# Rows gathered by index tile by tile, and attention heads in 8 and 16 bits over 128-row keys

## The chip, the cores and the metric

One core of one Trainium2 chip runs the whole kernel in one launch. The metric is the device time of that launch in microseconds; the kernel before takes 337.29 us (median of three runs, 334.5 to 338.93). The core has five engines with queues of their own that meet only at semaphores: PE (TensorE), DVE (VectorE), ACT (ScalarE), POOL (GpSimd) and SP (SyncE, which here issues DMAs only).

## The reference

Four residual blocks over x of 1024 tokens by 256; ctx is 4 x 256 x 256.

```python
x = x + experts(layernorm(x), token_ids, Wg=Wu=Wd=ctx)     # expert of a token from its id, clipped, // 3125
#   g = silu(h @ ctx[e].T); u = h @ ctx[e].T; y = (g * u) @ ctx[e].T
x = x + fp8(layernorm(x)) @ fp8(W8).T * scales              # e4m3, one scale per tensor, result in bf16
h = layernorm(x)
q = fq_sym(h @ Wq + bq, per head row); k, v = fq_sym(ctx @ Wkv + bkv)   # 16 heads of 16, 1024 keys, 8-bit grids
p = softmax(q k^T / 4); p = round(p / (max p / 255)) * (max p / 255)
x = x + (p @ v) @ Wp + bp
x = x + layernorm(x) @ ternary(Wt).T + bt
```

The probabilities are integers from 0 to 255 times a scale, so they can be held in 16 bits or in 8.

## The kernel before, in words

The order of all work is written out by hand: each engine has one block, and what an engine does next is the next line of its block, held back by `wait_ge` on semaphores.

**Sorting (0 to 36 us).** Tokens are counted per expert by small matmuls over masks, which give each token its place (`dest`). The token rows are loaded into `record`, POOL scatters them to a buffer in HBM in eight indirect DMAs (L369), and one DMA loads the sorted rows into `xs` (L314). PE meanwhile turns ctx and makes keys and values `kv` (L1022), DVE adds their bias (L695). The first layer norm follows for all eight tiles at once: sums on DVE (L684), root on POOL (L374, L375), norm on DVE (L703).

**Experts (36 to 86 us).** Eleven jobs: eight tiles of 128 sorted tokens, and three extra jobs for tiles in which an expert begins. A step of the loop over `s` holds, for different jobs, a transpose (L1039), the gate product (L1047), a sigmoid on ACT, two products on DVE (`zz`, `gu`), a transpose back (L1080), the second product, and the addition to `xs`. Between them DVE's `background(s)` prepares keys, values and weights, and the second norm's sums follow. POOL splits the keys into bf16 parts; its last product (`ksplit`, L401) signals `klo`, upon which SP turns the keys by eight DMA transposes into `keysT` (L321), where head 2j holds rows 0 to 63 and head 2j+1 rows 64 to 127.

**fp8 block and queries (86 to 129 us).** A maximum over all, quantising on DVE, a product, the third norm's sums (L850), its root on POOL (L374, four tiles at a time), norms, query products (L1158), their 8-bit grid, and transposes into `qT`.

**Attention (129 to 302 us).** For each of eight tiles and 16 heads: PE makes 128 x 1024 scores in two matmuls over the head's 64 rows (L1175) in one of three PSUM buffers, DVE reduces their maximum (L878), POOL makes the bias of the exponential (L421), ACT writes exp as int16 and its sum (L566), and so frees the buffer. For every pair of heads SP issues a DMA transpose of 2048 columns into `probT` (L331), and PE weighs the values, eight matmuls per head (L1204), six heads behind the scores. Once a tile DVE divides (L923), and POOL adds the output bias `bp` to a tile (L432) and copies the tile's scales to `qcur`.

**End (302 to 336 us).** Projection, fourth norm, ternary product, and eight scatters of the output.

## Time and profile before

| | us |
|---|---|
| runs: median (lowest to highest) | 337.29 (334.5 to 338.93) |
| profiled execution | 337.5 |
| its span, first to last instruction | 335.7 |
| PE / DVE / ACT / POOL busy | 268.7 / 265.7 / 210.0 / 98.3 |
| mean granted TensorE clock | 0.65 of full |

Busy time says how much of the span an engine computes, not which one holds up the others: PE and DVE are both near 80%. The strips of the page divide the span into 40 slices of 8.4 us; a digit 5 in the clock strip is the lower of TensorE's two levels (1.2 GHz), a 9 the upper one (2.4 GHz). The timeline gives each instruction's start and length, and in brackets how long its engine had been idle and what it waited for.

### The profile page before, as it was taken

The page shows a single profiled execution, that of the slowest core. Times are in us where ns is not written, and L with a number is a line of the kernel's source. Part 1 is how long each engine was busy: PE and PEld are TensorE (multiplying, and loading weights), DVE is VectorE, ACT ScalarE, POOL GpSimd, SP SyncE. Part 2 cuts the span into 40 slices and gives each one's busy share as a digit, 9 for nine tenths or more (in the row PEclk, how much of TensorE's full clock was granted, in tenths as well). Part 3 has the DMA queues.
Part 4 walks back from the last instruction along what each step waited for, and adds up shares of the span by engine and source line. Part 5 has one row for each costly group of instructions (what it writes and reads, how often), then busy time and mean ns, then how long its engine had stood idle before and what let it go on. Part 6 is the DMA issues. An engine that isn't in the chain of part 4 may idle for free.

```text
span 335.7 us, 5142 instructions
## 1 busy us (share of the span) xinstructions
PE 268.7 (80%) x1728; PEld 127.3 (38%) x1728; DVE 265.7 (79%) x401; ACT 210.0 (63%) x340; POOL 98.3 (29%) x225
## 2 busy tenths in 40 slices
PE   4993597595156947899999999999999999979670
PEld 4441365473034733233333332333333333338560
DVE  3363799968697878999999899899999999973850
ACT  1100125435533178999999999999999999992210
POOL 2350424476603011221222212222222122211634
PEclk9999559987555977555555555555555555558998
DMA  7824000039100001999999999999999999995011
GB/s 255 276 94 126 0 3 0 0 59 161 34 0 0 0 2 37 196 182 206 185 200 178 215 172 212 184 212 164 227 167 219 197 188 190 199 184 109 16 49 63
DMA packets 148618, 43.34 MB, mean 129 GB/s; under 512 B 143216, under 2 KB 147696, under 8 KB 148592
## 3 DMA queue, kind: packets, MB, share of 16 engines
q1 hardware_dynamic: 146496, 39.60, 65.4%
q0 software_dynamic: 768, 2.10, 1.8%
q10 hardware_dynamic: 1328, 1.32, 1.2%
q8 instruction: 14, 0.23, 0.3%
q14 instruction: 12, 0.10, 0.1%
HBM read 5.25 MB, written 2.10 MB: 22 GB/s over the span
## 4 chain that ended last, share of the span: by engine, by line
issue 36%; DVE 18%; PE 17%; POOL 16%; ACT 6%; DMA 6%; POOLq 1%; ACTq 0%; DVEq 0%
POOL ebias L421 8%; PE ps L1175 5%; PE ps L1158 4%; PE ps L1047 3%; DMA ksplit<-in_x 3%; DVE nmax L878 2%; ACT ctxT L566 2%; POOL scratch L369 2%; PE ps L1150 2%; POOL rstd L375 2%; POOL xs L432 2%; DMA xs<-scratch 2%; POOL out L446 1%; DVE stats L850 1%; ACT kv L557 1%
## 5 line engine op out<-in xcount | busy, mean ns | idle before, releaser
L878 DVE TENSOR_REDUCE nmax<-ps 128x1 f32<-128x1024 f32 x128 | 156.3, 1224 | 16.5 <-PE ps L1175 11.6
L1175 PE MATMUL ps<-keysT,kv 64*128 64x512 bf16 x256 | 130.1, 614 | 9.2 <-ACT ctx L566 1.9
L566 ACT ACTIVATE ctx<-ps,ebias,qscale 128x1024 int16<-128x1024 f32 x64 | 76.9, 1203 | 5.4 <-POOL ebias L421 3.5
L566 ACT ACTIVATE ctxT<-ps,ebias,qscale 128x1024 int16<-128x1024 f32 x64 | 77.0, 1203 | 4.0 <-POOL ebias L421 2.5
L1204 PEld LDWEIGHTS ps<-vals,ksplit 128*128 128x128 f16 x1024 | 36.9, 105 | 100.6 <-issue 100.3
L421 POOL TENSOR_SCALAR ebias<-nmax,qcur 128x1 f32<-128x1 f32 x128 | 33.8, 264 | 136.2 <-DVE nmax L878 127.2
L1204 PE MATMUL ps<-vals,ksplit 128*128 128x16 f16 x1024 | 47.7, 176 | 0.8 <-DVE krest L923 0.8
L475 ACT COPY hT<-ps 128x256 f32<-128x256 f32 x11 | 4.1, 372 | 46.5 <-PE ps L1039 46.5
L1175 PEld LDWEIGHTS ps<-keysT,kv 64*128 64x128 bf16 x256 | 16.3, 107 | 21.8 <-ACT ctx L566 8.1
L543 ACT COPY hT<-ps 128x512 f32<-128x512 f32 x8 | 4.7, 586 | 22.5 <-PE ps L1150 22.5
L1022 PE MATMUL ps<-wkv_s,ctxT 128*128 128x512 f32 x32 | 16.4, 668 | 0.7 <-ACT ctxT L469 0.7
L374 POOL TENSOR_SCALAR vareps<-mv 128x1 f32<-128x1 f32 (+3 forms) x15 | 3.9, 257 | 44.3 <-DVE mv L854 29.8
L1047 PE MATMUL ps<-ctxT,hT 128*128 (+1 forms) x44 | 15.5, 486 | 1.7 <-ACT hT L475 1.7
L1047 PE MATMUL ps<-ctxT,guT 128*128 (+1 forms) x44 | 13.3, 431 | 1.3 <-ACT guT L481 1.3
L375 POOL TENSOR_TENSOR rstd<-vareps,half 128x1 f32<-128x1 f32 (+3 forms) x15 | 12.5, 834 | 1.3
L566 ACT ACTIVATION_READ_ACCUMULATOR ctx<-ps,ebias,qscale 128x1 f32 x64 | 12.3, 192 | 0.0
L566 ACT ACTIVATION_READ_ACCUMULATOR ctxT<-ps,ebias,qscale 128x1 f32 x64 | 12.2, 191 | 0.0
L1047 PEld LDWEIGHTS ps<-ctxT,hT 128*128 128x128 f32 x44 | 10.2, 246 | 4.4 <-issue 2.8
L369 POOL DMA_INDIRECT scratch<-ksplit,dest x8 | 7.9, 992 | 12.3 <-DMA ksplit<-in_x 10.1
L695 DVE TENSOR_TENSOR kv<-ps,bkv_b 128x512 f32<-128x512 f32 x8 | 5.3, 683 | 7.3 <-PE ps L1022 6.6
L1039 PE MATMUL ps<-identf,hs 128*128 128x128 f32 x16 | 3.9, 331 | 8.8 <-DVE hs L703 8.8
L1080 PE MATMUL ps<-identf,gu 128*128 128x128 f32 x22 | 5.2, 324 | 7.0 <-DVE gu L768 7.0
(176 smaller groups left out, 316.1 us busy)
## 6 DMA issues: line engine op xcount, KB each, us to landing
ctx<-in_ctx SPq DMA_DIRECT2D x2, 512.0 KB, 4.9
ksplit<-in_x ACTq DMA_DIRECT2D x1, 1024.0 KB, 10.9
xs<-scratch SPq DMA_DIRECT2D x1, 1024.0 KB, 5.6
wkv_s<-in_L_xattn_Wkv SPq DMA_DIRECT2D x1, 512.0 KB, 8.1
ksplit<-ctx SPq DMA_TRANSPOSE x32, 4.7
ksplit<-ctxT SPq DMA_TRANSPOSE x32, 4.9
bkv_b<-in_L_xattn_bkv ACTq DMA_DIRECT2D x1, 256.0 KB, 11.4
wt_s<-in_L_ffn_weight SPq DMA_DIRECT2D x1, 256.0 KB, 9.4
```

The costliest lines, as they stand in the source:

```text
L369: g.indirect_dma_start(scratch, bass.IndirectOffsetOnAxis(ap=dest[:, t:t + 1], axis=0), record[:, t, :], None).then_inc(scattered, 16)
L375: root = g.tensor_tensor(rstd[:, lo:hi], vareps[:, lo:hi], half[:, 0:hi - lo], ALU.pow)
L421: g.tensor_scalar(ebias[:, slot], nmax[:, slot], qcur[:, u:u + 1], LN255, ALU.mult, ALU.add).then_inc(bias_ready, 1)
L432: g.tensor_tensor(xs[:, t, :], xs[:, t, :], bp_b[:, :], ALU.add).then_inc(x3b_ready, 1)
L566: a.activation(prob_of(w)[:, (u % 2) * NK:(u % 2 + 1) * NK], score_banks(k, u), ACT.Exp, bias=ebias[:, u % 4:u % 4 + 1], scale=qscale[:, t ...
L878: v.tensor_reduce(nmax[:, u % 4:u % 4 + 1], score_banks(k, u), AX.X, ALU.max, negate=True).then_inc(max_ready, 1)
L1022: last = m.matmul(ps[:, KVB[r % 4], :], ctxT[:, c, r * P:(r + 1) * P], wkv_s[:, c, :], start=(c == 0), stop=(c == C - 1))
L1047: last = m.matmul(ps[:, bank, 0:D], lhs[:, c, :], ctxT_e[:, c, e, :], start=(c == 0), stop=(c == C - 1))
L1150: last = m.transpose(ps[:, bank, k * P:(k + 1) * P], src[:, t, c * P:(c + 1) * P], identf[:, :])
L1158: last = m.matmul(ps[:, bank, i * D:(i + 1) * D], lhs[:, g % 2, i * C + c, :], w[:, c, :], start=(c == 0), stop=(c == C - 1))
L1175: last = m.matmul(ps[:, bank + b, :], qT[rows, t, u // 2, :], keysT[rows, u // 2, 512 * b:512 * b + 512], start=True, stop=True)
L1204: last = m.matmul(out, probT[:, (u // 2) % PAIRS, (u % 2) * KT + r, :].bitcast(F16), vals[:, r, u * HD:(u + 1) * HD], start=(r == 0), stop ...
```

## The change

It has four parts.

1. *Rows by index.* A second set of small matmuls turns `dest` into its inverse, `token_of`: the token at each sorted place. POOL then gathers `xs` tile by tile straight from x; load, scatter and reload are gone. The first norms are done tile by tile, three on DVE and five on ACT, and the experts start while kv products are still to come. ACT makes z squared beside the sigmoid, so one product on DVE gives the gate. The jobs are ordered five tiles, three extras, three tiles.
2. *8/16-bit heads.* The exponentials of even heads are written as bytes, two keys to a 16-bit word (so ACT reads PSUM with a step of 128 elements), those of odd heads as int16. A pair is then 1536 columns for the DMA transpose. POOL copies an even head's transposed bytes into 16-bit words (`byteT`, `unpack`), six heads behind, and PE weighs seven heads behind.
3. *Keys of 128 rows.* Each block of keys is turned twice into `keysT[:, a]`, and POOL clears the half that belongs to the other head of the pair (`keys_zeroed`), so that scores take all 128 rows. The roots of the third norm stand behind this on POOL. `klo` stands behind the second norm's roots.
4. *Unread transposes.* Before each head's weighing PE makes four 128 x 128 transposes of the identity into a free half of a bank that nobody reads (`FILLERS`). The output bias is added in two instructions ahead of the loop, and `qcur` is gone.

```diff
-FIRST_MAINS = 3
+FIRST_MAINS = 5
+EARLY_NORMS = 3
+ROOT_GROUPS = ((0, 1), (1, 3), (3, 5), (5, 7), (7, 8))
 QT_BY_DVE = (5, 7)
-KEY_PARTS = (4, 6)
-NORM_AT = 4
+KEY_PARTS = (7, 10)
+KV_FIRST = 5
 PARTS = 3
 PAIRS = 4
-WEIGH_LAG = 6
+PT = 4
+UNPACK_LAG = 6
+WEIGH_LAG = 7
+FILLERS = 4
...
-                sp.dma_start_transpose(keysT[:, :, r * P:(r + 1) * P],
-                                       ksplit[:, r * H:(r + 1) * H, :, :].rearrange("p a s d -> p (a s d)")).then_inc(
-                                           keys_turned[r], 16)
+                for a in range(2):
+                    sp.dma_start_transpose(keysT[:, a, :, r * P:(r + 1) * P],
+                                           ksplit[:, r * H:(r + 1) * H, :, :].rearrange("p a s d -> p (a s d)")).then_inc(
+                                               keys_turned[r], 16)
...
-            pool.wait_ge(dest_ready, 1)
-            pool.wait_ge(ld_x, 16)
-            for t in range(NT):
-                g.indirect_dma_start(scratch, bass.IndirectOffsetOnAxis(ap=dest[:, t:t + 1], axis=0),
-                                     record[:, t, :], None).then_inc(scattered, 16)
+            def gather(t):
+                g.indirect_dma_start(xs[:, t, :], None, x_rows,
+                                     bass.IndirectOffsetOnAxis(ap=token_of[:, t:t + 1], axis=0)).then_inc(gathered[t], 16)
...
+            pool.wait_ge(token_ready, 1)
+            for t in range(3):
+                gather(t)
+            for k, (lo, hi) in enumerate(ROOT_GROUPS):
+                first_root(lo, hi)
+                for t in range(2 * k + 3, min(2 * k + 5, NT)):
+                    gather(t)
...
+            for t in range(0, NT, 2):
+                pool.wait_ge(sums2_ready, t + 2)
+                inverse_root(t, t + 2)
+                for i in range(t, t + 2):
+                    g.tensor_scalar(nmr[:, i:i + 1], mv[:, i, 0:1], rstd[:, i:i + 1], -1.0,
+                                    ALU.mult, ALU.mult).then_inc(rstd2, 1)
             pool.wait_ge(kmid, 2)
             g.tensor_tensor(ksplit[:, :, 2, :], k3, ksplit[:, :, 1, :], ALU.subtract).then_inc(klo, 1)
-            for t in range(NT):
-                pool.wait_ge(sums2_ready, t + 1)
-                inverse_root(t, t + 1)
-                g.tensor_scalar(nmr[:, t:t + 1], mv[:, t, 0:1], rstd[:, t:t + 1], -1.0,
-                                ALU.mult, ALU.mult).then_inc(rstd2, 1)
             pool.wait_ge(wide_used, 5)
             g.tensor_tensor(vq[:, :, :], kv[:, :, D:2 * D],
                             vinv[:, :].unsqueeze(1).broadcast_to([P, KT, D]), ALU.mult).then_inc(vn_ready, 1)
 
+            pool.wait_ge(vn_ready, 1)
+            for r in range(KT):
+                pool.wait_ge(keys_turned[r], 32)
+                for a in range(2):
+                    if r + a:
+                        pool.wait_ge(keys_zeroed, 2 * r + a)
+                    other = slice(P // 2, P) if a == 0 else slice(0, P // 2)
+                    g.memset(keysT[other, a, :, r * P:(r + 1) * P].bitcast(F32), 0.0).then_inc(keys_zeroed, 1)
+
+            pool.wait_ge(keys_zeroed, 2 * KT)
...
+            def unpack(t, u):
+
+                pair_turned(pool, t, u // 2)
+                if not (first_tile(t) and u < 2 * PT):
+                    pool.wait_ge(pv_done, count(*before(t, u, 2 * PT)))
+                g.tensor_copy(byteT[:, (u // 2) % PT, :, :, :],
+                              rawT[:, (u // 2) % PAIRS, 0:KT // 2, :].bitcast(U8).rearrange(
+                                  "p b (q j) -> p b j q", j=2)).then_inc(unpacked, 1)
+
             def attention(t, k):
-                if not first_tile(t):
-                    pool.wait_ge(bias_ready, t * H)
-                g.tensor_copy(qcur[:, :], qscale[:, t, :]).then_inc(qcur_ready, 1)
-                pool.wait_ge(qcur_ready, t + 1)
                 for u in range(H):
                     exp_bias(t, u)
-                    if u == H // 2:
-                        g.tensor_tensor(xs[:, t, :], xs[:, t, :], bp_b[:, :], ALU.add).then_inc(x3b_ready, 1)
...
+            def gates(j):
+
+                act.wait_ge(z_full, j + 1)
+                if j >= 2:
+                    act.wait_ge(gu_ready, j - 1)
+                a.activation(sig[:, j % 2, :], ps[:, j % 2, 0:D], ACT.Sigmoid).then_inc(gates_ready, 1)
+                a.activation(square[:, j % 2, :], ps[:, j % 2, 0:D], ACT.Square).then_inc(gates_ready, 1)
...
+                if u % 2 == 0:
+                    probs = prob_of(w)[:, 0:NK // 2].bitcast(U8).rearrange("p (b q j) -> p b q j", q=P, j=2)
+                    s_in = score_banks(k, u).rearrange("p (b j q) -> p b q j", j=2, q=P)
...
+            pe.wait_ge(ids_ready, 2)
+            for t in range(NT):
+                last = m.matmul(ps[:, 4, 0:2 * NT], at_lane[:, t, :], ids[:, t, :, :].rearrange("p i t -> p (i t)"),
+                                start=(t == 0), stop=(t == NT - 1))
+            last.then_inc(tokens_full, 1)
...
-                rows = slice(u % 2 * P // 2, (u % 2 + 1) * P // 2)
                 for b in range(2):
-                    last = m.matmul(ps[:, bank + b, :], qT[rows, t, u // 2, :], keysT[rows, u // 2, 512 * b:512 * b + 512],
+                    last = m.matmul(ps[:, bank + b, :], qT[:, t, u // 2, :], keysT[:, u % 2, u // 2, 512 * b:512 * b + 512],
...
-            def weigh(t, k, u):
-
-                pair_turned(pe, t, u // 2)
+            def weigh(t, k, u, fillers=True):
+
+                if u % 2 == 0:
+                    pe.wait_ge(unpacked, t * NP + u // 2 + 1)
+                else:
+                    pair_turned(pe, t, u // 2)
                 if u == 0 and k % NS == 0 and not first_tile(t):
                     pe.wait_ge(att_ready, t)
                 if u == 0 and k % NS == 2:
                     pe.wait_ge(att_ready, t - 1)
+                if fillers:
+                    idle = ps[:, PV_BANKS[k % NS], D:2 * D].bitcast(BF16)
+                    for i in range(FILLERS):
+                        m.transpose(idle[:, i * P:(i + 1) * P], identb[:, :], identb[:, :])
                 out = ps[:, PV_BANKS[k % NS], u * HD:(u + 1) * HD]
                 for r in range(KT):
-                    last = m.matmul(out, probT[:, (u // 2) % PAIRS, (u % 2) * KT + r, :].bitcast(F16), vals[:, r, u * HD:(u + 1) * HD],
+                    if u % 2 == 0:
+                        probT = byteT[:, (u // 2) % PT, r // 2, r % 2, :]
+                    else:
+                        probT = rawT[:, (u // 2) % PAIRS, KT // 2 + r, :]
+                    last = m.matmul(out, probT.bitcast(F16), vals[:, r, u * HD:(u + 1) * HD],
                                     start=(r == 0), stop=(r == KT - 1))
```

On POOL, from the last root of the second norm up to the first biases, this stood before:

```order
L374 TENSOR_SCALAR vareps<-mv 128x1
L375 TENSOR_TENSOR rstd<-vareps,half 128x1
L405 TENSOR_SCALAR nmr<-mv,rstd 128x1
L408 TENSOR_TENSOR vq<-kv,vinv 128x2048
L374 TENSOR_SCALAR vareps<-mv 128x4
L375 TENSOR_TENSOR rstd<-vareps,half 128x4
L374 TENSOR_SCALAR vareps<-mv 128x4
L375 TENSOR_TENSOR rstd<-vareps,half 128x4
L427 COPY qcur<-qscale 128x16
L421 TENSOR_SCALAR ebias<-nmax,qcur 128x1 x9
L432 TENSOR_TENSOR xs<-xs,bp_b 128x256
```

The same stretch of POOL's order now, with L443 the product that signals `klo`, L455 the clearing of the keys and L476 the unpacking:

```order
L393 TENSOR_SCALAR vareps<-mv 128x2
L394 TENSOR_TENSOR rstd<-vareps,half 128x2
L440 TENSOR_SCALAR nmr<-mv,rstd 128x1 x2
L443 TENSOR_TENSOR ksplit<-krest,ksplit 128x128x16
L445 TENSOR_TENSOR vq<-kv,vinv 128x2048
L455 MEMSET keysT 64x8x64 x16
L393 TENSOR_SCALAR vareps<-mv 128x4
L394 TENSOR_TENSOR rstd<-vareps,half 128x4
L393 TENSOR_SCALAR vareps<-mv 128x4
L394 TENSOR_TENSOR rstd<-vareps,half 128x4
L490 TENSOR_TENSOR xs<-xs,bp_b 128x1024 x2
L468 TENSOR_SCALAR ebias<-nmax,qscale 128x1 x7
```

The product behind `klo` and sixteen clearings have come in between the second norm's roots and the third norm's; the bias addition has moved ahead of the loop.

On PE, in the attention loop (L1300 scores, L1332 the unread transposes, L1339 the weighing of an even head from `gates`, where `byteT` lies, and of an odd one from `ksplit`):

```order
L1300 MATMUL ps<-keysT,kv 128x512 x18
L1332 MATMUL ps<-identb 128x128 x4
L1339 MATMUL ps<-vals,gates 128x16 x8
L1300 MATMUL ps<-keysT,kv 128x512 x2
L1332 MATMUL ps<-identb 128x128 x4
L1339 MATMUL ps<-vals,ksplit 128x16 x8
```

Before, two score matmuls and eight weighing matmuls alternated; now four transposes stand ahead of each eight.

## Rows read from the trace of the kernel before

**Rows 1.** The page's strips, 40 slices of the span: VectorE busy tenths, TensorE clock tenths.

```profile
DVE  3363799968697878999999899899999999973850
PEclk9999559987555977555555555555555555558998
```

**Rows 2.** Table by stretches: us, each engine busy (instructions), clock, DMA share, GB/s.

```profile
127.50:128.00 0.50, 0.50 (x10) 0.50 (x8) 0.50 (x2) 0.21 (x1) 0.00 (x0) 0.76 0.00 0
...
131.00:131.50 0.50, 0.03 (x1) 0.00 (x0) 0.50 (x2) 0.50 (x2) 0.10 (x1) 0.65 0.00 0
...
180.00:200.00 20.00, 19.43 (x148) 6.06 (x144) 18.44 (x17) 18.94 (x31) 4.79 (x17) 0.50 1.16 182
```

**Rows 3.** Timeline of one head: start, length, engine, line, operation, count, idle before.

```profile
221.14 1.03 PE L1175 MATMUL ps<-keysT,kv 64*128 64x512 bf16 x2
...
222.22 1.23 DVE L878 TENSOR_REDUCE nmax<-ps 128x1 f32<-128x1024 f32 x1 [0.25 <-PE ps L1175]
...
222.42 1.03 PE L1175 MATMUL ps<-keysT,kv 64*128 64x512 bf16 x2
...
223.53 0.26 POOL L421 TENSOR_SCALAR ebias<-nmax,qcur 128x1 f32<-128x1 f32 x1 [1.21 <-DVE nmax L878]
...
223.83 1.20 ACT L566 ACTIVATE ctxT<-ps,ebias,qscale 128x1024 int16<-128x1024 f32 x1 [0.18 <-POOL ebias L421]
...
225.18 1.03 PE L1175 MATMUL ps<-keysT,kv 64*128 64x512 bf16 x2
```

**Rows 4.** Timeline, ends of the loop, and first and last of POOL's eight additions.

```profile
129.07 1.21 ACT L566 ACTIVATE ctx<-ps,ebias,qscale 128x1024 int16<-128x1024 f32 x1
...
130.27 1.20 ACT L566 ACTIVATE ctx<-ps,ebias,qscale 128x1024 int16<-128x1024 f32 x1
...
139.82 0.72 POOL L432 TENSOR_TENSOR xs<-xs,bp_b 128x256 f32<-128x256 f32 x1
...
291.60 0.72 POOL L432 TENSOR_TENSOR xs<-xs,bp_b 128x256 f32<-128x256 f32 x1
...
302.45 2.82 PE L1150 MATMUL ps<-identf,krest 128*128 128x128 f32 x12 [2.05 <-ACT ctxT L566]
```

**Rows 5.** Ahead of the loop: timeline; kv's row is from the groups by line.

```profile
10.93 5.74 PE L1022 MATMUL ps<-wkv_s,ctxT 128*128 128x512 f32 x8 [0.72 <-ACT ctxT L469]
...
L1022 PE MATMUL ps<-wkv_s,ctxT 128*128 128x512 f32 x32 | 16.4, 668 | 0.7 <-ACT ctxT L469 0.7
...
41.06 0.42 DVE L765 TENSOR_TENSOR zz<-ps,sig 128x256 f32<-128x256 f32 x1 [2.26 <-ACT sig L505]
...
83.83 0.18 DVE L785 BATCH_NORM_AGGREGATE mv<-stats 128x2 f32<-128x6 f32 x1
...
85.30 4.49 POOL L408 TENSOR_TENSOR vq<-kv,vinv 128x2048 f32<-128x2048 f32 x1
...
102.59 0.58 POOL L374 TENSOR_SCALAR vareps<-mv 128x4 f32<-128x4 f32 x1 [12.80 <-DVE mv L854]
```

**Rows 6.** Timeline around the clock's rise: query transposes, scores, two maxima.

```profile
125.65 2.92 PE L1190 MATMUL ps<-identb,ksplit 128*128 128x128 bf16 x32
...
129.45 0.59 PE L1175 MATMUL ps<-keysT,kv 64*128 64x512 bf16 x2 [0.88 <-DVE kv L911]
...
130.08 2.36 DVE L878 TENSOR_REDUCE nmax<-ps 128x1 f32<-128x1024 f32 x2 [0.77 <-PE ps L1175]
```

**Rows 7.** Groups by line on POOL: busy us, mean ns of one, idle before.

```profile
L387 POOL COPY extra_h<-hs 128x256 f32 x3 | 1.2, 399 | 4.4 <-DVE hs L703 3.8 <-issue 0.5
...
L388 POOL COPY extra_mask<-extra 128x1 f32 x3 | 0.6, 186 | 0.0
```

**Rows 8.** SP's key transposes: ns min/median/max, first and last start; time to landing.

```profile
L321 SPq DMA_TRANSPOSE keysT<-ksplit x8: 1327/1340/2431, 71.8 to 81.4; - x8
...
DMA to landing us min/median/max: 3.3/3.3/5.0
```

**Rows 9.** Groups by line on VectorE: the reduce that reads with a step.

```profile
L720 DVE TENSOR_REDUCE vmax<-kv 128x128 f32<-128x1024 f32 x2 | 3.9, 1943 | 0.1
```

More of the change, by code:

```diff
@@ L420, in exp_bias @@
                 slot = slice(u % 4, u % 4 + 1)
-                g.tensor_scalar(ebias[:, slot], nmax[:, slot], qcur[:, u:u + 1], LN255,
+                g.tensor_scalar(ebias[:, slot], nmax[:, slot], qscale[:, t, u:u + 1], LN255,
                                 ALU.mult, ALU.add).then_inc(bias_ready, 1)
+            def unpack(t, u):
[5 more added lines that the diff above has]
+                                  "p b (q j) -> p b j q", j=2)).then_inc(unpacked, 1)
             def attention(t, k):
-                if not first_tile(t):
-                    pool.wait_ge(bias_ready, t * H)
-                g.tensor_copy(qcur[:, :], qscale[:, t, :]).then_inc(qcur_ready, 1)
-                pool.wait_ge(qcur_ready, t + 1)
                 for u in range(H):
                     exp_bias(t, u)
-                    if u == H // 2:
-                        g.tensor_tensor(xs[:, t, :], xs[:, t, :], bp_b[:, :], ALU.add).then_inc(x3b_ready, 1)
+                    if u % 2 == 0 and not (first_tile(t) and u < UNPACK_LAG):
+                        unpack(*before(t, u, UNPACK_LAG))
             pool.wait_ge(ld_b, 48)
+            for k in range(2):
+                part = slice(k * NT // 2, (k + 1) * NT // 2)
+                pool.wait_ge(h3_ready, (k + 1) * NT // 2)
+                g.tensor_tensor(xs[:, part, :], xs[:, part, :], bp_b[:, :].unsqueeze(1).broadcast_to([P, NT // 2, D]),
+                                ALU.add).then_inc(x3b_ready, 1)
+            pool.wait_ge(x3b_ready, 2)
             pool.wait_ge(qinv_ready, 2)
@@ L447, in scatter_output @@
                                          x4[:, t, :], None).then_inc(stored, 16)
+            for u in range(H - UNPACK_LAG, H, 2):
+                unpack(NT - 1, u)
             fourth_root(0)
-            pool.wait_ge(ld_order, 16)
             fourth_root(1)
@@ L467, in _ @@
             for g in range(2):
-                act.wait_ge(ctxT_full, 2 * g + 2)
-                a.copy(ctxT[:, 1, 512 * g:512 * g + 512], ps[:, 2 * g + 1, :]).then_inc(ctxT_by_act, 1)
+                for c in range(C):
+                    act.wait_ge(ctxT_full, 2 * g + c + 1)
+                    a.copy(ctxT[:, c, 512 * g:512 * g + 512], ps[:, 2 * g + c, :]).then_inc(ctxT_ready, 1)
             def copy_hT(j):
@@ new lines, in add_kv, with first_sums, first_norm @@
+            def add_kv(r):
+                dve.wait_ge(kv_full, r + 1)
+                v.tensor_tensor(kv[:, r, :], ps[:, KVB[r % 2], :], bkv_b[:, :], ALU.add).then_inc(kv_ready, 1)
+            def first_sums(t):
+                dve.wait_ge(gathered[t], 16)
+                step(v.bn_stats(stats[:, t, :], xs[:, t, :]))
+                v.bn_aggr(mv[:, t, :], stats[:, t, :]).then_inc(sums1_ready, 1)
+            def first_norm(t):
+                dve.wait_ge(rstd_ready, 1 if t == 0 else 2)
@@ new lines, in _ @@
+            weights(3)
+            first_norm(1)
+            first_norm(2)
+            add_kv(4)
+            kk = kv[:, :, 0:D].rearrange("p r (h d) -> p r h d", d=HD)
+            def background(s):
+                for t in ((3,), (4, 5), (6,), (7,))[s] if s < 4 else ():
+                    first_sums(t)
+                if s < KT - KV_FIRST:
+                    add_kv(s + KV_FIRST)
+                if s == 5:
+                    weights(KT - 1)
+                if s == 3:
+                    dve.wait_ge(kv_ready, KT)
@@ L985, in _, with turn_ctx @@
                      stop=True).then_inc(ranks_full, 1)
-            for g in range(2):
+            def turn_ctx(g):
                 pe.wait_ge(ld_ctx[g], 16)
@@ L1181, in _ @@
                     pe.wait_ge(qT_by_act, NT // 2)
-                    for r in range(KT):
-                        pe.wait_ge(keys_turned[r], 16)
+                    pe.wait_ge(keys_zeroed, 2 * KT)
                     for u in range(2):
```

314 lines of the change are left out of this document (181 added, 133 removed).

## Prediction

> **What bounds the kernel now.** I read the two strips of the page first: over the last two thirds VectorE sits at 9 tenths or just under and the granted TensorE clock at 5 tenths [rows 1]. The table by stretches says the same of 180 to 200 us: TensorE, VectorE and ScalarE are all over 90% busy, the clock is at its lower level (1.2 GHz), and the DMA share is over 1 [rows 2]. Four resources nearly full together is usually a ring, so I followed one head through the timeline [rows 3]. Scores start at 221.14 and take 1.03; the maximum starts at 222.22 and takes 1.23; the bias starts at 223.53; the exponential at 223.83; the scores three heads later, which need its PSUM buffer, start at 225.18. That is 4.04 us for three heads, 1.347 each. The eight tiles' `xs` additions on POOL are 21.68 us apart ((291.60 - 139.82)/7), 1.355 per head [rows 4]. So **the loop runs at the latency of the three score buffers**, and no engine alone explains it. Inside it TensorE also needs 1.28 per head (221.14 to 222.42): it has almost no room at the low clock.
>
> The loop goes from the first exponential at 129.07 to 302.4 [rows 4]; what lies ahead of it is one long chain through the experts (first gate 41.06, last statistics 84.0), the fp8 product and the queries, whose POOL root (the third norm's) starts at 102.59 [rows 5].
>
> **The loop, part by part.** *Clock.* Warm, the same two score matmuls took 0.59 (129.45) instead of 1.03 [rows 6]: 0.43 off each turn of the ring. Is it warm afterwards? The clock rose during 127.5 to 128.0, after two unbroken microseconds of 128-row bf16 transposes, held to about 131, fell with 64-row scores, and never rose again although TensorE was 97% busy [rows 2, 6]. The change makes the scores 128 rows and puts four 128-column transposes into each head. At the low clock that is 1.28 + 4 x 0.107 = 1.71 us of work per head (an estimate: 128 columns at 1.2 GHz; the 32 transposes at 125.65 took 2.92, 0.09 each, at both levels [rows 6]), more than a turn leaves, so TensorE would be full until the clock rises; warm it needs about 0.9. I take the clock as risen. The rule against it stands in the Trainium skill, page "TensorE: Matmul & The Clock Gate", section Part 4: transposes do not count as busy for the clock. By that rule the fillers only add work, and the sum would be the first rival's 381; the rise at 127.5 came in a run of nothing but transposes [rows 6] and speaks against it.
>
> *Ring.* 4.04 - 0.43 = 3.61, 1.204 per head. ScalarE's own pace is 1.20 (129.07 to 130.27) and VectorE's about 1.13 (two maxima in 2.36) [rows 4, 6], so all three bounds lie together.
>
> *Unpacking.* POOL gets a 1024-element byte-to-16-bit copy behind each even head's bias. No row has it. Low bound: POOL copies at 399 ns for 256 elements and 186 for one, 0.835 ns per element, so 1.04 us. High bound: its two-input rate, 4.49 for 2048 elements, so 2.25 us [rows 5, 7]. It has one input and is nearest to the copy: 1.04. Then POOL is held 0.26 + 1.04 + 0.1 = 1.4 after an even head's bias starts, and the odd head's bias comes 0.2 late; a ring turn pair holds one such, (2 x 3.61 + 0.2)/6 = 1.24 per head. The 0.72 us addition and the `qcur` copy leave POOL's loop and are in that difference. The DMA carries 12 blocks per pair instead of 16; a transpose of 8 blocks is issued every 1.38 us (71.8 to 81.4, seven steps) and lands after 3.3 to 5.0 [rows 8], so 12 take about 2.1 of the pair's 2.48, where 16 would take 2.75 and become the bound. Behind late transposes POOL, then the next bias, would wait; the byte copy has 5 heads (about 5 us behind the exponential) for a landing near 4.
>
> *Even heads' exponential* reads PSUM with a step and writes bytes. I take 1.20 as now; the nearest stepped read is VectorE's `vmax` at 1943 ns against 1.23 us for a contiguous maximum over as many elements [rows 3, 9], the other end.
>
> Loop: heads with weighing behind them gain (1.355 - 1.24) x 121 = **-13.9**; the first seven I leave as they are.
>
> **Ahead of the loop.** The 1 MB load into `record`, eight scatters and the reload go; gathers feed tile by tile. The first gate, at 41.06 now, then waits for kv products instead: they start about 11.7 (10.93 now plus the token matmuls), five of them at 2.05 (16.4 for eight) end at 22, and product and gates bring it to 26 [rows 5]: 15 us earlier. From there VectorE drops 11 `zz` at 0.42 and takes over five tiles' statistics and three kv additions, about even; extras, which wait for the last tile's norm, cost 1.5. The last statistics come at 84.0 - 13.5 = 70.5.
>
> But **a new wait eats this**. On POOL `klo` now stands behind the second norms' roots. Now POOL goes from the last statistics to its next large product in 1.3 (84.0 to 85.30), for a pair of tiles I add one 0.3, and the product of 2048 elements takes up to 4.49 [rows 5]: 70.5 + 1.6 + 4.5 = 76.6. SP then issues 16 key transposes, not 8: the last starts 15 x 1.38 = 20.7 later and lands 3.3 to 5.0 after, at 100.6 to 102.3 [rows 8]; POOL clears its half twice (512 elements, 0.6 each by its copy rate), at 101.8 to 103.5. The root of the third norm is queued behind all of them, and hs, queries and first scores behind that root. It started at 102.59; now 102.8: **+0.2**. The 15 us vanish, and VectorE, ScalarE and TensorE idle for some 13 us before 103. The two bias additions on POOL (half a tile set each) lie beside the query products.
>
> **After the loop**: twelve transposes at the low clock took 2.82 [rows 4]; at a risen clock about **-0.8** of the chain goes. Three late unpacks hide beside the first projections.
>
> Against the profiled execution's 337.5 (span 335.7 plus 1.8 around it; it is 0.2 above the median of the runs, 337.29): 337.5 + 0.2 - 13.9 - 0.8 = **323.0**.
>
> **The rivals.**
> 1. *The clock stays low or falls back.* Each head costs TensorE 1.71: 337.5 + 0.2 + (1.71 - 1.355) x 121 = 381. It decides from where fewer than three quarters of the heads are warm ((1.71 - 1.355)/(1.71 - 1.24)). For it: 97% busy at the low clock for 170 us. Against: the rise at 127.5. 9%.
> 2. *The stepped exponential costs like the stepped reduce*: even heads 1.20 + 0.72, so 3.12 per pair, 1.56 per head, (1.56 - 1.355) x 128 = +26, less 0.6: 363. It turns to a loss where an even head's exponential passes about 1.5 us. Nothing in the trace reads PSUM so; 7%. The Trainium skill, page "Advanced Engine Details and Errata", section PSUM Cachelines, gives PSUM lines of 8 bytes, asks that every two consecutive elements be contiguous, and says that matmuls slow down otherwise; carried over to ScalarE's reads, this rival would be the forecast and the time 363.
> 3. *The unpack is dear.* At 1.5 us the odd bias is 0.6 late, (7.22 + 0.6)/6 = 1.30, 331; at 2.25 POOL itself needs 2.9 per pair, 1.45 per head, 348. The gain ends near 1.9 us. 17%, two thirds of it above 330.
> 4. *The front does gain*, because transposes go out faster or `klo` is earlier: up to 10 us, 313. The cadence of 1.38 was steady over eight, so 7%.
>
> **The numbers.** The forecast has 60%, alone 316 to 330. Leaving out rivals 1 and 2 (16%) and a corner of the others gives the range 314 to 342. Two per cent either way, about what a measurement tells from no change, is 330.5 to 344. Faster: forecast, rival 4 and a third of rival 3, 0.71; within: the rest of the forecast's edge and most of rival 3, 0.11; slower: rivals 1, 2 and the dearest unpack, 0.18.
>
> **What the changed profile would show.** Clock strip at 9 in the loop, score pairs at about 0.6 us, head pace 1.24, ScalarE's idle almost none. An unpack row near 1.04 us and odd heads' biases waiting for it. ScalarE's two forms both at 1.20. SP's 16 key transposes from about 77 to 99, POOL's third root at about 103, with VectorE idle ahead of it, and the first exponential at about 129 as before. A clock at 5 in the loop, an even-head exponential over 1.5, or a first exponential near 119 would each make the prediction wrong.

## The result, and the profile after

The changed kernel takes **346.64 us** (median of four runs, 344.24 to 347.51) against 337.29 before: a ratio of 1.0268, 95% interval 1.0223 to 1.0314, slower. Forecast were 323.0 and a range of 314 to 342. The profiled execution took 347.51, its span 345.4.

The strips of the page after, VectorE's busy tenths and TensorE's clock:

```profile
DVE  3574549978792578798998999998999999892941
PEclk9989969878555686787999999999999999999996
```

Against [rows 1] the clock strip has turned from 5 to 9 in the loop, as forecast. The loss shows in VectorE's row: a 2 and a 5 at the thirteenth and fourteenth slices (104 to 121 us), ahead of the loop. The timeline of POOL and VectorE there:

```profile
83.45 4.06 POOL L443 TENSOR_TENSOR ksplit<-krest,ksplit 128x2048 bf16<-128x2048 f32 x1
...
111.76 1.09 POOL L455 MEMSET keysT<- 64x512 f32 x2 [1.61 <-DMA keysT<-ksplit]
112.95 0.24 POOL L393 TENSOR_SCALAR vareps<-mv 128x4 f32<-128x4 f32 x1
...
105.32 0.25 DVE L952 BATCH_NORM_AGGREGATE mv<-stats 128x2 f32<-128x6 f32 x2
114.41 1.38 DVE L942 TENSOR_SCALAR hs<-xs,mv,rstd 128x256 f32<-128x256 f32 x4 [8.85 <-POOL rstd L394]
```

The third norm's root starts at 112.95, not at 102.59 [rows 5]; VectorE had idled 8.85 us for it. It is the wait that the prediction named (a root queued behind clearings, which wait for key transposes, which wait for `klo`), but ten microseconds later than it was put. The sixteen transposes themselves are as forecast, in the view of their line:

```profile
L339 SPq DMA_TRANSPOSE keysT<-ksplit x16: 1320/1338/1387, 87.6 to 108.4; - x16
DMA to landing us min/median/max: 3.3/3.4/4.2
```

The first exponential starts at 143.19 (129.07 before), the last ends at 313.09 (302.30), and the tail behind it takes 32.3 (33.4). So the span's +9.7 is **+14.1 ahead of the loop, -3.3 in it, -1.1 behind it**; forecast were +0.2, -13.9 and -0.8.

The two forms of ScalarE's exponential, from the groups by form, and the unpacking's own line:

```profile
L644 ACT ACTIVATE ctxT<-ps,ebias,qscale 128x1024 int16<-128x1024 f32 x32 | 38.5, 1204 | 3.5 <-POOL ebias L468 2.7
L644 ACT ACTIVATE ctxT<-ps,ebias,qscale 128x1024 uint8<-128x1024 f32 x32 | 38.3, 1196 | 0.2 <-POOL ebias L468 0.2
```

```profile
L476 POOL CAST gates<-ksplit x64: 1036/1036/1041, 150.7 to 317.2; 128x1024 int16<-128x1024 uint8 x64
its engine sat idle before it (us, times) until:
  DMA ksplit<-ctxT: 5.1, 5
  DMA ksplit<-ctx: 2.3, 4
```

The stepped read of PSUM costs nothing, the unpacking takes the 1.04 that was taken for it, and nine times POOL sat idle for its transposes, 7.4 us in all: six times in the loop (4.1) and three times behind the last exponential (3.3).

One pair of heads in the loop (ACT, POOL and PE's scores, with the maximum between):

```profile
222.79 0.26 POOL L468 TENSOR_SCALAR ebias<-nmax,qscale 128x1 f32<-128x1 f32 x1 [0.77 <-DVE nmax L976]
223.12 1.04 POOL L476 CAST gates<-ksplit 128x1024 int16<-128x1024 uint8 x1
223.26 1.20 ACT L644 ACTIVATE ctxT<-ps,ebias,qscale 128x1024 uint8<-128x1024 f32 x1
223.41 0.60 PE L1300 MATMUL ps<-keysT,kv 128*128 128x512 bf16 x2 [0.38 <-ACT ctx L644]
224.25 0.26 POOL L468 TENSOR_SCALAR ebias<-nmax,qscale 128x1 f32<-128x1 f32 x1
224.54 1.21 ACT L644 ACTIVATE ctxT<-ps,ebias,qscale 128x1024 int16<-128x1024 f32 x1
```

Scores take 0.60 where they took 1.03 [rows 3]. The odd head's bias (224.25) starts when the unpacking ends, and its exponential 1.28 behind the even one. Over the loop the starts repeat 1.28, 1.20, 1.39, 1.20: 1.267 a head where nothing else disturbs.

### The profile page after: what moved, and what is told of

Same layout as the page of the kernel before. It is cut to its first block, busy times and chain, and to the rows that moved or that the text cites. A ratio compares the mean times of both kernels' runs of the same rounds, so it can differ in the third digit from the quotient of the medians.

```text
span 345.4 us, 6285 instructions
## 1 busy us (share of the span) xinstructions
PE 230.3 (67%) x2220; PEld 158.5 (46%) x2220; DVE 267.3 (77%) x390; ACT 211.9 (61%) x358; POOL 172.9 (50%) x299
## 4 chain that ended last, share of the span: by engine, by line
issue 31%; POOL 25%; PE 15%; DVE 14%; SPq 6%; ACT 4%; DMA 3%; POOLq 1%; DVEq 0%
POOL gates L476 13%; POOL ebias L468 7%; SPq L339 6%; PE ps L1284 3%; PE ps L1127 2%; PE ps L1156 2%; PE ps L1177 2%; DMA xs<-in_x,token_of 2%; DVE gates L865 2%; POOL rstd L394 1%; DVE hs L942 1%; ACT ctxT L644 1%; PE ps L1314 1%; POOL ksplit L443 1%; PE ps L1276 1%
## 5 line engine op out<-in xcount | busy, mean ns | idle before, releaser
L1300 PE MATMUL ps<-keysT,kv 128*128 128x512 bf16 x256 | 79.8, 395 | 42.6 <-ACT ctx L644 22.2
L644 ACT ACTIVATE ctx<-ps,ebias,qscale 128x1024 uint8<-128x1024 f32 x64 | 76.7, 1200 | 7.7 <-POOL ebias L468 6.5
L644 ACT ACTIVATE ctxT<-ps,ebias,qscale 128x1024 uint8<-128x1024 f32 x64 | 76.6, 1200 | 3.7 <-POOL ebias L468 2.9
L468 POOL TENSOR_SCALAR ebias<-nmax,qscale 128x1 f32<-128x1 f32 x128 | 33.9, 265 | 81.5 <-DVE nmax L976 75.0
L476 POOL CAST gates<-ksplit 128x1024 int16<-128x1024 uint8 x64 | 66.3, 1037 | 10.8 <-DMA ksplit<-ctxT 5.1
L1332 PEld LDWEIGHTS ps<-identb 128*128 128x128 bf16 x484 | 37.8, 100 | 29.6 <-issue 2.4
L1332 PE MATMUL ps<-identb 128*128 128x128 bf16 x484 | 47.7, 222 | 0.3 <-POOL gates L476 0.3
L1300 PEld LDWEIGHTS ps<-keysT,kv 128*128 128x128 bf16 x256 | 14.8, 98 | 58.0 <-ACT ctx L644 29.3
L1339 PE MATMUL ps<-vals,gates 128*128 128x16 f16 x512 | 22.4, 170 | 0.0
L1339 PE MATMUL ps<-vals,ksplit 128*128 128x16 f16 x512 | 22.3, 170 | 0.0
L1339 PEld LDWEIGHTS ps<-vals,gates 128*128 128x128 f16 x512 | 19.7, 97 | 0.1
L1339 PEld LDWEIGHTS ps<-vals,ksplit 128*128 128x128 f16 x512 | 19.7, 97 | 0.1
L455 POOL MEMSET keysT<- 64x512 f32 x16 | 8.6, 535 | 12.3 <-DMA keysT<-ksplit 11.9
```

Source lines behind the costliest of these rows:

```text
L468: g.tensor_scalar(ebias[:, slot], nmax[:, slot], qscale[:, t, u:u + 1], LN255, ALU.mult, ALU.add).then_inc(bias_ready, 1)
L476: g.tensor_copy(byteT[:, (u // 2) % PT, :, :, :], rawT[:, (u // 2) % PAIRS, 0:KT // 2, :].bitcast(U8).rearrange("p b (q j) -> p b j q", j= ...
L644: a.activation(probs, s_in, ACT.Exp, bias=ebias[:, u % 4:u % 4 + 1], scale=qscale[:, t, u:u + 1], accum_out=lsum[:, t, u:u + 1]).then_inc( ...
L1300: last = m.matmul(ps[:, bank + b, :], qT[:, t, u // 2, :], keysT[:, u % 2, u // 2, 512 * b:512 * b + 512], start=True, stop=True)
L1332: m.transpose(idle[:, i * P:(i + 1) * P], identb[:, :], identb[:, :])
L1339: last = m.matmul(out, probT.bitcast(F16), vals[:, r, u * HD:(u + 1) * HD], start=(r == 0), stop=(r == KT - 1))
```

## The experiments

All are the changed kernel with one thing different, unless said otherwise. Times are medians; ratios are to the kernel before, with 95% intervals. "First exponential" is its start in the profiled execution. Between executions of the same code the front (what lies ahead of the loop) itself varies by some microseconds, as G and L show, so it is read there by its steps.

**A. Keys of 64 rows again.** Four unread transposes a head stay; each block is turned once and nothing is cleared.

```diff
-                for a in range(2):
-                    sp.dma_start_transpose(keysT[:, a, :, r * P:(r + 1) * P],
+                sp.dma_start_transpose(keysT[:, :, r * P:(r + 1) * P],
...
+                rows = slice(u % 2 * P // 2, (u % 2 + 1) * P // 2)
                 for b in range(2):
-                    last = m.matmul(ps[:, bank + b, :], qT[:, t, u // 2, :], keysT[:, u % 2, u // 2, 512 * b:512 * b + 512],
+                    last = m.matmul(ps[:, bank + b, :], qT[rows, t, u // 2, :], keysT[rows, u // 2, 512 * b:512 * b + 512],
```

> The changed kernel with its keys as before (64 rows, each block turned once, nothing cleared); the four unread transposes stay. Theory (the unread transposes hold the clock, the 128 rows do not matter): clock 1.00 in the loop, score pair 0.60 us, the loop as now (170 us from the first to the last exponential); the front loses 8 transposes and the clearings, the third root starts at about 104 instead of 112.95, and the time is about 337. Rival (it is the 128 rows that bring the clock up): clock 0.50, 1.71 us of TensorE work per head, a loop of 215 us or more, a time of 385.

Measured: 382.72 us, 1.1344 (1.1252 to 1.1436). By stretches (columns as in [rows 2]):

```profile
200.00:240.00 40.00, 40.00 (x334) 20.02 (x333) 29.26 (x27) 30.93 (x49) 18.77 (x36) 0.50 0.70 113
```

The rival holds. TensorE is full at 0.50, and the exponentials are 1.70 or 1.71 apart except around the division: the prediction's 1.71 for a cold head, and near its rival's 381. What it had not priced is that, with the transposes in place, the rows of the scores decide between the two. The front did as the theory says: third root at 103.42, first exponential at 130.88.

**B. No unread transposes.** `FILLERS = 0`.

> The changed kernel without the unread transposes; the 128-row keys stay. Theory (the unread transposes hold the clock): clock 0.5, score pair 1.03 us, 1.36 to 1.40 us per head as before the change, a loop of 177 us and a time of 354. Rival (128-row scores suffice): clock 1.00, the loop at 170 or a little less, time 345 to 347.

Measured: 355.33 us, 1.0521 (1.0427 to 1.0615).

```profile
160.00:200.00 40.00, 33.80 (x292) 16.75 (x291) 35.41 (x34) 36.26 (x58) 22.82 (x44) 0.59 0.85 143
200.00:240.00 40.00, 30.00 (x291) 15.40 (x290) 35.88 (x33) 36.96 (x59) 23.09 (x45) 0.76 0.83 145
```

The loop takes 175.6, near the theory's 177, but not at a steady low clock: it swings (0.59, 0.76). So neither part 3 nor part 4 holds the clock alone here; together they do (1.00 from 165 to 311 us, with TensorE 76% busy). The Trainium skill, page "TensorE: Matmul & The Clock Gate", section Part 4, says that transposes do not count as busy for the clock. A agrees with it; B, 355 without the transposes against 346.6 with them, does not.

**C. Unpacking in two halves**, one behind each bias (each half copies half of the blocks).

```diff
-                    if u % 2 == 0 and not (first_tile(t) and u < UNPACK_LAG):
-                        unpack(*before(t, u, UNPACK_LAG))
+                    if not (first_tile(t) and u < UNPACK_LAG):
+                        unpack(*before(t, u - u % 2, UNPACK_LAG), u % 2)
```

> The changed kernel with each unpacking cut into two halves, one behind each bias. Theory (the 1.04 us unpacking behind an even head's bias makes the odd head's bias late, 1.28 and 1.39 between these exponentials instead of 1.20): a half takes 0.55, no bias is late, the undisturbed pace goes from 1.267 to 1.20 to 1.22, the loop from 170 to 162 or 164, the time to 339 to 341. Rival (VectorE is the bound: 16 maxima of 1.225, the division 0.43 and the reciprocal 0.24 per tile are 20.3 us, 1.267 per head): no change, 346.

Measured: 337.88 us, 1.0019 (0.9974 to 1.0063), where the changed kernel had 1.0268. ScalarE and POOL in the loop:

```profile
222.66 0.26 POOL L468 TENSOR_SCALAR ebias<-nmax,qscale 128x1 f32<-128x1 f32 x1 [0.25 <-DVE nmax L978]
222.99 0.61 POOL L477 CAST gates<-ksplit 128x512 int16<-128x512 uint8 x1
222.97 1.19 ACT L646 ACTIVATE ctx<-ps,ebias,qscale 128x1024 uint8<-128x1024 f32 x1
224.16 1.19 ACT L646 ACTIVATE ctx<-ps,ebias,qscale 128x1024 int16<-128x1024 f32 x1
```

POOL now waits for the maximum, no longer the bias for POOL. Starts are 1.18 to 1.24 apart, 1.20 on average; the loop takes 163.5, 6.4 less than in the changed kernel. (Of the 8.9 between the two profiled executions another 2.6 lie in the front, whose code is the same.) Three gaps of 1.48 to 2.05 for late transposes are left of six. The one gap that every tile but the first still has is 2.0 long, at the ninth head, where VectorE waits 0.44 for the last head's weighing and divides for 0.42.

**D. Third norm's roots ahead of the clearings.**

```diff
+            for k in range(2):
+                pool.wait_ge(sums3_ready, k + 1)
+                inverse_root(k * NT // 2, (k + 1) * NT // 2, rstd3)
+            pool.wait_ge(rstd3, 2)
             pool.wait_ge(vn_ready, 1)
             for r in range(KT):
...
             pool.wait_ge(keys_zeroed, 2 * KT)
-            for k in range(2):
-                pool.wait_ge(sums3_ready, k + 1)
-                inverse_root(k * NT // 2, (k + 1) * NT // 2, rstd3)
```

> The changed kernel with the third norm's two roots ahead of the sixteen clearings on POOL. Theory (the front's loss is a queue on POOL: the third root waits at 112.95 us behind clearings that wait for the key transposes): the statistics it needs are complete at 103.9, so the root starts there, 9 us earlier; the first exponential goes from 143.2 to about 134 and the time falls by about 9, to 337 or 338. Rival (the clearings only move the wait: the queries are written over the keys and wait for the last key transpose, landed at 111.8, and the bias additions behind the clearings reach to 124): the root moves by 9 but the first exponential by less than 5.

Measured: 337.52 us, 0.9987 (0.9942 to 1.0032). Root at 104.03, first exponential at 133.01: theory. The clearings had no need to stand first; in the changed kernel TensorE takes the keys 25 us after they end (112.9, 137.8).

**E. `klo` early.** `KEY_PARTS = (7, 9)`, and POOL's product behind the first group of the second norm's roots.

```diff
                 for i in range(t, t + 2):
                     g.tensor_scalar(nmr[:, i:i + 1], mv[:, i, 0:1], rstd[:, i:i + 1], -1.0,
                                     ALU.mult, ALU.mult).then_inc(rstd2, 1)
-            pool.wait_ge(kmid, 2)
-            g.tensor_tensor(ksplit[:, :, 2, :], k3, ksplit[:, :, 1, :], ALU.subtract).then_inc(klo, 1)
+                if t == 0:
+                    pool.wait_ge(kmid, 2)
+                    g.tensor_tensor(ksplit[:, :, 2, :], k3, ksplit[:, :, 1, :], ALU.subtract).then_inc(klo, 1)
```

> The changed kernel with the second key part cut one step earlier on ScalarE (steps 7 and 9) and the product that signals klo behind the first of the second norm's four groups of roots on POOL instead of the last. Theory: klo is done near 79 instead of 87.5, the sixteen transposes run from 79 to 99.5 and the third root starts at about 104 instead of 112.95, held then by its own statistics; first exponential 134 to 135, time about 338. Rival (POOL's product of 4.06 us holds up the second norm's roots and with them the fp8 product): the second norm ends 2 to 3 us later, the statistics of the third come at 106 or later, and only 5 to 6 us are gained, 341.

Measured: 338.15 us, 0.9989 (0.9947 to 1.0031). The product runs from 74.24 to 78.30, transposes start at 78.39, the third root at 104.67, the first exponential at 133.34. The same 10 us come back by another door; the second norm's last statistics are 1.6 later (83.2), too little for the rival.

**F. Bias additions behind all third norms.**

```diff
-                pool.wait_ge(h3_ready, (k + 1) * NT // 2)
+                pool.wait_ge(h3_ready, NT)
```

> The changed kernel with both output-bias additions on POOL waiting for all eight third norms, not the first for four. Theory (the addition and VectorE's four norms of one SBUF operand get in each other's way: 3.39 us for four norms at 118.96, where the same four took 1.38 at 114.41): the four take 1.38, the first exponential comes 2 us earlier and the time is 344.5. Rival (it then meets the query stage's VectorE instructions instead): the same 2 us are lost there, 346.5.

Measured: 345.71 us, 1.0203 (1.0119 to 1.0286). Not to be told from the changed kernel's 1.0268, but the traces show what happens. First the changed kernel, then this one:

```profile
118.89 2.34 POOL L490 TENSOR_TENSOR xs<-xs,bp_b 128x1024 f32<-128x1024 f32 x1
118.96 3.39 DVE L942 TENSOR_SCALAR hs<-xs,mv,rstd 128x256 f32<-128x256 f32 x4 [1.50 <-POOL rstd L394]
```

```profile
119.43 1.38 DVE L942 TENSOR_SCALAR hs<-xs,mv,rstd 128x256 f32<-128x256 f32 x4 [1.49 <-POOL rstd L394]
120.95 5.52 POOL L490 TENSOR_TENSOR xs<-xs,bp_b 128x1024 f32<-128x1024 f32 x2 [1.56 <-DVE hs L942]
124.63 1.90 DVE L992 TENSOR_SCALAR qscale<-qmax 128x64 f32<-128x64 f32 x1
```

The norms are down to 1.38, and L992, 0.20 long in the changed kernel (127.77), lasts 1.90: until 126.53, where POOL's additions end (126.47). The stall has moved, as the rival says: of the 2.0 won in the norms it takes back 1.7. The first exponential is earlier all the same, at 141.18, and 27.75 behind the root where it was 30.24. That is not the edit's doing alone: the second group's query products took 1.89 at the higher clock, not 3.08, which is 1.6 on VectorE's path, and the last 32 transposes 2.64, not 3.22. C, with the stall of 3.40 in place, has the 1.89 too.

**G. The gate as before**, two products that read PSUM, no Square on ScalarE.

```diff
-                v.tensor_tensor(gu[:, j % 2, :], square[:, j % 2, :], sig[:, j % 2, :], ALU.mult).then_inc(gu_ready, 1)
+                step(v.tensor_tensor(square[:, j % 2, :], ps[:, j % 2, 0:D], sig[:, j % 2, :], ALU.mult))
+                v.tensor_tensor(gu[:, j % 2, :], ps[:, j % 2, 0:D], square[:, j % 2, :], ALU.mult).then_inc(gu_ready, 1)
```

> The changed kernel with the gate as before: two products on VectorE that each read z from PSUM, and no Square on ScalarE. Theory (the single gate product, both operands in SBUF, waits for POOL's large products: 3.97 us at 64.05 during L434, where the others take 0.42): that stall of 3.5 goes, 8 further products of 0.42 cost about 2 of it on the path, klo comes 1.5 to 3 us earlier and the time is 344 to 345. Rival (a stall of VectorE there is hidden by ScalarE and TensorE, or an equal stall hits the next SBUF instruction): 346 to 348.

Measured: 340.54 us, 1.0073 (1.0024 to 1.0122), a larger gain than was expected. Its profiled execution took 345.8 and showed no earlier front (last statistics at 81.92), so it was profiled once more:

> The kernel with the gate read from PSUM once more, for a profile of a usual execution (340) in place of one at 345.8. Theory (the blocked gate product delayed the second norm): last statistics before 81, klo and the third root 2 to 4 us earlier than 113. Rival (the front is unchanged, first exponential at 143, and the 5 us lie elsewhere, in the loop's first tile or the clock).

Measured: 342.08 us, one run. Last statistics at 79.21 (81.61 in the changed kernel), third root at 110.60, first exponential at 136.98. The blocked product is real (rows below). From the fourth gate to the last it is 33.0 us in the changed kernel (40.59 to 73.55), 30.9 in the first profile of G and 30.2 in the second: its removal gives 2.1 to 2.7. The first profile had lost 1.9 of that ahead of the fourth gate (42.66 against 40.77), with kv products at the lower clock (2.71 against 1.88). Of the second's 6.2 us at the first exponential, 2.4 are there at the root; the other 3.9, from the root on, belong to nothing that the edit touches. TensorE's products and transposes there ran at the higher clock in this execution where in the changed kernel's they did not (the second group's query products 1.89 against 3.08, the last 32 transposes 1.95 against 3.22). Of the timed gain of 6.1, then, 2 to 3 us are explained; the rest is open.

**H. Six tiles ahead of the extra jobs.** `FIRST_MAINS = 6`, with the sums' steps adapted.

> The changed kernel, with six tiles ahead of the three extra jobs as its only difference. Theory (the experts' expected 13.5 us shrank to 2.2 because three jobs wait: 3.4 each for a gathered tile's norm and for the extra copies, 3.5 for the blocked gate product): the second 3.4 go, the last statistics move from 81.6 to about 79, klo and the third root with them, time 344. Rival (VectorE's total of work up to the last statistics, 9 to 10 of 10 us busy from 55 to 85, sets the end): unchanged, 346.5.

Measured: 341.51 us, 1.0124 (1.0018 to 1.0231). Last statistics at 77.76 instead of 81.61, third root at 108.89, 4.1 earlier; first exponential at 137.54, 5.7 earlier (here too the second group's query products took 1.89).

**I. All heads in 16 bits**, 16 blocks per transpose, no unpacking.

```diff
-    PW = NK + NK // 2
+    PW = 2 * NK
...
-                if u % 2 == 0:
-                    probs = prob_of(w)[:, 0:NK // 2].bitcast(U8).rearrange("p (b q j) -> p b q j", q=P, j=2)
...
-                    probs, s_in = prob_of(w)[:, NK // 2:PW], score_banks(k, u)
+                probs, s_in = prob_of(w)[:, u % 2 * NK:(u % 2 + 1) * NK], score_banks(k, u)
```

> The changed kernel with all heads in 16 bits again (no stepped exponential, no unpacking, 16 blocks per transpose); 128-row keys and unread transposes stay. Theory (the transposes then set the pace: eight blocks take 1.38 us, sixteen 2.75 per pair, 1.375 a head): a loop of 176 us, time 352. Rival (the transposes keep up, and with no unpacking the loop runs at ScalarE's 1.20): a loop of 156 to 160, time 334 to 337.

Measured: 348.50 us, 1.0298 (1.0212 to 1.0384). Landings of its transposes, and a stretch:

```profile
DMA to landing us min/median/max: 4.3/5.0/7.0
```

```profile
240.00:260.00 20.00, 14.47 (x205) 9.96 (x205) 18.41 (x17) 18.10 (x31) 4.23 (x16) 1.00 1.22 199
```

Between the two. In the profiled execution (352.0, above the median) the exponentials run 1.20 apart, and once or twice a tile wait 0.4 to 1.7 for a late landing; the loop takes 170.3. Sixteen blocks can keep 2.4 us a pair for a while. The theory's 2.75, twice the issue time of eight, was too slow, and the trace of the kernel before could have told: its transposes of sixteen blocks are issued in 2.15 to 2.19 (medians) and land after 4.7. But late landings take back what the missing unpacking gives. In the changed kernel eight bits therefore bought little or nothing (348.50 against 346.64). By these profiles they pay once the unpacking is out of the bias's way: C's loop takes 163.5.

**J. The terms together**: C, E, F, G, the last block's clearing behind the first root, and the weighing's bank by tile with the division one head later.

```diff
-                if u == 0 and k % NS == 0 and not first_tile(t):
-                    pe.wait_ge(att_ready, t)
-                if u == 0 and k % NS == 2:
+                if u == 0 and t >= 2:
                     pe.wait_ge(att_ready, t - 1)
...
-                out = ps[:, PV_BANKS[k % NS], u * HD:(u + 1) * HD]
+                out = ps[:, 6 + t % 2, u * HD:(u + 1) * HD]
...
-DIVIDE_AT = 8
+DIVIDE_AT = 9
```

> The changed kernel with the undone waits together: klo early, the last block's clearing behind the third norm's first root, bias additions behind all third norms, the gate from PSUM, unpacking in halves, and one thing more: the weighing's PSUM bank alternates by tile (6, 7) and VectorE divides one head later, so that it does not wait for the last head's weighing. Theory, the terms add up: front -10, bias additions -2, gate 0 to -5, halves -8.5, division 0.45 a tile, -3: 318 to 323. Rival (VectorE and ScalarE are so near to full that the loop's terms do not add, 1.25 per head whatever is done): 327.

Measured: 325.11 us, 0.9624 (0.9550 to 0.9698). First exponential at 131.75, a loop of 159.0, 19.5 to 19.6 per undisturbed tile, 1.22 a head; the gap at the division is down from 2.0 to 1.46.

**K. J with six tiles first.**

> The combined kernel with six tiles ahead of the three extra jobs, not five. Theory (an extra job's copy waits for the last tile's norm, and TensorE, in order, waits with it: 4.8 us before 45.75 in the changed kernel): the wait overlaps one more tile's work, the statistics of the second norm end 2 to 3 us earlier and the time is 2 to 3 below the combined kernel's. Rival (the later jobs only shift, VectorE's own work sets the end): within 1 us of it.

Measured: **323.01 us, 0.9593 (0.9499 to 0.9686)**, faster than the kernel before. First exponential at 128.27, the loop 160.2. That the time equals the forecast's 323.0 is chance and no support for it: this kernel has seven changes that the forecast's does not.

**L. K with two unread transposes a head.**

> The combined kernel with six tiles first, and two unread transposes per head instead of four. Theory (any steady run of 128-row work holds the clock, and 128-row scores already half hold it): clock 1.00 in the loop, same 323. Rival (the amount counts: without any, the granted clock swung between 0.59 and 0.76): clock near 0.8, time 326 to 330.

Measured: 325.48 us, 0.9661 (0.9601 to 0.9721). The clock between 160 and 280 us is 0.96 to 1.00 in stretches of 40 us, as in K, and the loop takes 159.4, against K's 160.2: two hold it about as well as four. The intervals of K and L overlap; what their profiled executions differ by lies ahead of the loop (last statistics at 82.15, K's at 80.00; first exponential 132.24 and 128.27), whose code is the same.

## Why the prediction was wrong

From 323.0 to the profiled 347.5: 10.2 up to the third root, 3.8 from there to the first exponential, 10.6 in the loop, less 0.3 behind it, and 0.3 around the span.

**Up to the third root: the mechanism was right, the step "the last statistics come at 84.0 - 13.5 = 70.5" failed.** They came at 81.8. Everything behind held: 1.7 to the product, 4.06 for it (4.5 was put), 20.8 of transposes, 3.4 of landing, a pair of clearings, and the root. D and E each remove one link and each get the 10 us back. The start's gain was carried to the end of the experts as if their pace stayed; VectorE's rows in the changed kernel show who slows them:

```profile
29.28 0.43 DVE L865 TENSOR_TENSOR gates<-gates 128x256 f32<-128x256 f32 x1 [1.92 <-issue]
36.70 0.43 DVE L865 TENSOR_TENSOR gates<-gates 128x256 f32<-128x256 f32 x1 [3.37 <-ACT gates L542]
48.93 0.43 DVE L865 TENSOR_TENSOR gates<-gates 128x256 f32<-128x256 f32 x1 [3.37 <-ACT gates L542]
64.05 3.97 DVE L865 TENSOR_TENSOR gates<-gates 128x256 f32<-128x256 f32 x1
```

The first gate is 3.3 later than put: TensorE was idle for 3.2 us before 22.96, for which the profile names no releaser, and then, in order, had the fifth tile's four kv products before the gate's, 3.20 us from 23.44 (1.88 for four at the higher clock, 27.55). Then 3.4 for the fourth tile's norm, whose root is made together with the fifth's, behind both tiles' statistics. Then 3.4 for the extra copies, which need the last tile's norm (the sum had 1.5 for them); a main tile's gate was held too, since TensorE's transpose of the extra job stands ahead of its product. H moved that wait and won 3.9, which shows it. And 3.55 in one gate product, where both operands had moved from PSUM to SBUF: G shows it, 2.1 to 2.7 net of eleven more products. Less that 1.5, the four come to 12.2 where 11.3 are missing; they are waits read one by one, and no run separates the first two.

**From the root to the first exponential: a term put at nothing cost 2.0.** "The two bias additions on POOL (half a tile set each) lie beside the query products", said the prediction, and gave them no price. The first lies beside the last four norms, 3.39 instead of 1.38 (F). The rest, 1.8, is TensorE at the lower clock: 0.75 in VectorE's wait for the second group's query products (3.08 against 1.89), 1.35 in transposes and first scores (3.57, 3.22 and 1.89 us against 2.92, 2.92 and 1.04, in part overlapped), less 0.35 won before the norms. The clock was higher there in other executions (C, G), so I take this for no lasting term.

**In the loop** the clock, the scores at 0.6, the exponential and the unpacking were all right, and the sum was not. (a) The undisturbed pace is 1.267 and not 1.24 (sum of the ring and the late bias): every odd bias is late, where the sum had one late bias in two turns of the ring; 0.027 x 121 = 3.3. C removes it, and the pace is then 1.20, three heads in the 3.6 that the ring was put at. (b) The division was in 1.355, a measured tile average, and not in 1.24, built from one undisturbed head. The heads behind it go on at the usual pace and do not win it back. Six of them (tiles 3 to 8) show as gaps of 1.77 to 2.00, 11.13 together, 3.45 above 1.28 each. (c) "The byte copy has 5 heads (about 5 us behind the exponential) for a landing near 4" holds for the median, 3.7, but landings reach 5.9, and POOL holds biases behind the copy, here for 1.17:

```profile
186.15 1.04 POOL L476 CAST gates<-ksplit 128x1024 int16<-128x1024 uint8 x1 [1.17 <-DMA ksplit<-ctx]
187.58 1.20 ACT L644 ACTIVATE ctx<-ps,ebias,qscale 128x1024 int16<-128x1024 f32 x1 [1.11 <-POOL ebias L468]
```

Six gaps of 1.68 to 2.39, 11.85 together, 3.85 above 1.33 each (between 1.28 and 1.39). 3.3 + 3.45 + 3.85 = 10.6. What is left cancels: four gaps of 1.49 to 1.62 in the first tile cost about 1 us, and slightly faster heads elsewhere give it back. (a) is shown by C, and (b) by J, whose gap there is 1.46; (c) was read from the waits, not tried alone. Why single transposes land late stays open. (That twelve blocks would take about 2.1 to issue was wrong without effect: the median is 1.43.)

**The rivals.** The first (clock low) has its price confirmed by A; it comes true where the scores stay at 64 rows, and in part where the transposes are missing (B). The second (stepped read) fell: 1.196 against 1.204. The Trainium skill, page "Advanced Engine Details and Errata", section PSUM Cachelines, asks for contiguous pairs for matmuls; carried over to ScalarE's read, as the prediction tried, it does not hold here. The page itself speaks of matmuls only. The third (dear unpacking) fell by its duration but was right in kind: in one piece behind an even head's bias, even 1.04 makes every odd bias late. None of them held the way in which it was slower: several small terms of one sign, in the front and in a loop with VectorE and ScalarE at 92 and 93% (165 to 311 us).

## What to carry to other kernels

Do not carry an earlier start to the end of a stage by subtraction: list what each later step now waits for, in its own engine's order, for there the gain is lost first. On a queue that stands on the critical path, put what nobody needs yet behind what somebody waits for, and cut a long side job to less than the slack between two short ones. A loop's new pace must come from a whole tile with its once-a-tile work, and the tighter the ring, the more of that work and of late transfers shows in full.

## What the runs showed of the hardware

**VectorE behind POOL.** Some VectorE instructions on SBUF operands last until POOL's two-input product ends. Two such pairs in the changed kernel, POOL and VectorE:

```profile
55.97 3.79 POOL L431 TENSOR_TENSOR krest<-kq,kscale 128x2048 f32<-128x2048 f32 x1 [6.43 <-DVE kq L816]
57.36 2.41 DVE L824 TENSOR_SCALAR nthr<-thr 128x2 f32<-128x2 f32 x1
...
63.68 4.06 POOL L434 TENSOR_TENSOR krest<-krest,ksplit 128x2048 f32<-128x2048 f32 x1 [3.92 <-ACT ksplit L567]
```

L824, two elements wide, ends at 59.77, the product at 59.76; the gate product of 64.05 above ends at 68.02, L434 at 67.74. In G, where the gate reads PSUM, it stays at 0.42 beside the same product. The Trainium skill, page "SBUF — State Buffer", section "SBUF: two separate sides", has the rule: VectorE and GpSimd share a pair of ports that one of them holds for a whole instruction, VectorE in its 2-port modes or with two SBUF inputs. The rows agree, 3.97 beside 4.06. Not every instruction is held: the reduction before L824, with one input, took 0.69 at 56.64, beside L431.

**The clock in the loop**, by the rows of the score matmuls and the unread transposes per head: 64 and none 0.50 [rows 2]; 64 and four 0.50 (A); 128 and none 0.59 to 0.76 (B); 128 and two, and 128 and four, 0.96 to 1.00 (L and K; the changed kernel 1.00). TensorE was 95 to 100% busy in the first two and 73 to 85% in the others.

**The byte-to-16-bit copy on POOL** takes 1.036 us for 1024 elements and 0.61 for 512: cutting it costs 0.18.
